# Cross-attention of a two-layer decoder: input rows normalised by ScalarE instead of VectorE, mean and root prepared as two-tensor products

## The reference

```python
q_in = _layernorm(decoder_hidden, gamma, beta)
kv_in = _layernorm(encoder_output, gamma, beta)
q = q_in @ Wqkv[:D_MODEL].T
k = kv_in @ Wqkv[D_MODEL:2 * D_MODEL].T
v = kv_in @ Wqkv[2 * D_MODEL:].T
...
scores = jnp.einsum('bhqd,bhkd->bhqk', q, k) * SCALE
scores = scores + _temporal_bias(L_q, L_kv)[None, None, :, :]
attn = jax.nn.softmax(scores, axis=-1)
attended = jnp.einsum('bhqk,bhkd->bhqd', attn, v)
attended = attended.transpose(0, 2, 1, 3).reshape(B, L_q, D_MODEL)
attended = attended @ Wout.T + b_out
gate = jax.nn.sigmoid(attended @ Wgate.T + b_gate)
output = gate * attended + (1.0 - gate) * residual
```

## Time and profile before

| what | value |
|---|---|
| median of 3 runs | 2562.7 us (2561.79 to 2567.87) |
| the profiled execution | 2562.45 us, span of its instructions 2560.6 us |
| busy in the span: TensorE, VectorE, ScalarE, GpSimd | 2133.6, 1537.1, 949.2, 926.3 us |
| the stage of the change | about 1579 to 2364 us of the span |
| mean granted TensorE clock | 0.878 of full speed |

### The profile page before, as it was taken

The page is one execution under the profiler, slowest core; times in us unless marked ns, Lnnn a source line. Parts: engine busy times, 40 slices in busy tenths (PEclk is TensorE's granted clock), DMA queues, the critical chain, the costliest instruction groups (busy, mean ns, idle before and its releaser), DMA issues. The chain is left out here.

```text
span 2560.6 us, 58413 instructions
## 1 busy us (share of the span) xinstructions
PE 2133.6 (83%) x20310; PEld 1601.6 (63%) x20310; DVE 1537.1 (60%) x3500; ACT 949.2 (37%) x1881; POOL 926.3 (36%) x911
## 2 busy tenths in 40 slices
PE   5999997999776664888399996899999999997575
PEld 4666665777676563665398885566666666664233
DVE  0344443555454455333244654699999999984798
ACT  0444442333211110333124341344444444442797
POOL 0111111111144545232554531355555555553333
PEclk9999998999887776899677887899999999997555
DMA  6011003656311110876322311011000110000111
GB/s 207 26 30 30 29 25 116 217 198 215 132 50 32 37 35 24 271 241 182 92 86 78 102 39 39 26 32 32 26 28 30 32 32 30 24 20 8 53 57 46
DMA packets 157644, 192.76 MB, mean 75 GB/s; under 512 B 28517, under 2 KB 141160, under 8 KB 157559
## 3 DMA queue, kind: packets, MB, share of 16 engines
q1 hardware_dynamic: 136426, 179.73, 22.5%
q10 hardware_dynamic: 10861, 9.30, 1.2%
q0 software_dynamic: 10272, 2.62, 0.5%
HBM read 140.74 MB, written 77.51 MB: 85 GB/s over the span
## 5 line engine op out<-in xcount | busy, mean ns | idle before, releaser
L2730 ACT ACTIVATE xa_prob<-xa_A 121x1600 f32<-121x1600 f32 x96 | 144.5, 1505 | 304.2 <-PE xa_A L2609 304.2
L2801 POOL TENSOR_TENSOR xa_prob<-xa_prob,xa_exp_bias 121x1600 f32<-121x1600 f32 x64 | 228.7, 3574 | 41.0 <-ACT xa_prob L2730 40.9
L2908 DVE TENSOR_REDUCE xa_kq<-xa_A 100x4 f32<-100x1444 f32 x128 | 211.6, 1653 | 20.8 <-PE xa_A L2582 20.6
L1408 POOL DMA_INDIRECT slot_rows<-rt_x_again,rt_slot_u x150 | 151.9, 1012 | 163.8 <-DVE rt_x_again L1526 102.1
L2888 DVE TENSOR_SCALAR xa_rows_n<-xa_rows_t,xa_mv,xa_rstd 121x256 f32<-121x256 f32 x128 | 142.4, 1172 | 2.4 <-POOL xa_rstd L2818 2.4
L2609 PEld LDWEIGHTS xa_A<-xa_q2T,xa_kqT 17*121 17x121 f32 x3072 | 93.8, 185 | 56.5 <-DVE xa_kq L2908 35.9
L2582 PE MATMUL xa_A<-xa_kqT 16*100 16x361 f32 x1024 | 112.9, 510 | 10.0 <-ACT xa_prob L2730 6.8
L2609 PE MATMUL xa_A<-xa_q2T,xa_kqT 17*121 17x100 f32 x3072 | 109.3, 280 | 13.8 <-DVE xa_kq L2908 13.2
L695 DVE TENSOR_REDUCE sa_kq<-sa_A 100x16 f32<-100x1600 f32 x32 | 58.5, 1827 | 102.8 <-PE sa_A L453 102.8
L1654 POOL DMA_INDIRECT contrib<-ex_y,ex_place_u x64 | 62.4, 975 | 154.3 <-ACT ex_y L1706 135.5
L2823 POOL TENSOR_TENSOR xa_o_rstd<-xa_o_var,xa_power 100x1 f32<-100x1 f32 x32 | 17.9, 560 | 252.1 <-DVE xa_o_var L2948 252.1
(11 more groups left out here) (345 smaller groups left out, 5439.6 us busy)
## 6 DMA issues: line engine op xcount, KB each, us to landing
ex_w<-in_w13T SPq DMA_DIRECT2D x64, 352.0 KB
contrib<-xs_zero SPq DMA_DIRECT2D x30, 640.0 KB
la_rows<-contrib SPq DMA_DIRECT2D x16, 1200.0 KB
xs_ctxT<-in_ctxT SPq DMA_DIRECT2D x32, 512.0 KB
xa_rows_t<-in_ctx SPq DMA_DIRECT2D x96, 121.0 KB
ex_w<-in_w2T SPq DMA_DIRECT2D x64, 176.0 KB
slot_rows<-xs_zero SPq DMA_DIRECT2D x32, 272.0 KB
ex_x_t<-slot_rows SPq DMA_DIRECT2D x64, 136.0 KB, 2.2
```

Of the source, the lines that this page charges most:

```text
L1408: nc.gpsimd.indirect_dma_start(slot_rows, bass.IndirectOffsetOnAxis(slot_u[:, k, n:n + 1], 0), x_again[:, k, :], None, bounds_check=SLOTS ...
L2730: nc.scalar.activation(prob[:, n, :].rearrange("p (h a) -> p h a", h=HPG), A[:ROWS, :, 0:G * T], ACT.Exp, scale=EXP_SCALE).then_inc(exp_re ...
L2801: nc.gpsimd.tensor_tensor(chunk, chunk, exp_bias[:, n, :].unsqueeze(1).to_broadcast([ROWS, HEADS, T]), ALU.mult).then_inc(biased, 1)
L2908: nc.vector.tensor_reduce(kq[:T, k, NCH, 4 * j:4 * j + 4, DH:DH + 1].rearrange("p h o -> p (h o)"), A[:T, :, 0:src_len], axis=AXIS_X, op=A ...
```

## The change

The four operations of `normalise` move from VectorE to ScalarE, as an Identity activation with `rstd` as scale and a new tile `shift` as bias. VectorE prepares `shift` = -mean x root: `nmean` (zero minus mean) in `moments`, and the product with the root in `centre`, which stands where `normalise` stood. `var` becomes a sum of two tensors, the variance and a tile filled with epsilon, instead of a tensor and a number. On ScalarE `normalise(b+3)` stands between `y_out(b-1)` and `exponential(b, 2)`. GpSimd fills two small constant tiles once.

```diff
--- before.py
+++ after.py
@@ -2412,6 +2412,10 @@
         mv = s.sb("mv", [ROWS, LOTS, 2])
         var = s.sb("var", [ROWS, LOTS])
         rstd = s.sb("rstd", [ROWS, LOTS])
+        nmean = s.sb("nmean", [ROWS, LOTS])
+        shift = s.sb("shift", [ROWS, LOTS])
+        nothing = s.sb("nothing", [ROWS, LOTS])
+        ln_eps = s.sb("ln_eps", [ROWS, LOTS])
         power = s.sb("power", [ROWS, LOTS])
         o_stats = s.sb("o_stats", [T, 6])
         o_mv = s.sb("o_mv", [T, 2])
@@ -2428,7 +2432,8 @@
         loaded = [s.sem(f"loaded{k}") for k in range(2)]
         res_loaded = [s.sem(f"res_loaded{k}") for k in range(2)]
         stored = [s.sem(f"stored{k}") for k in range(2)]
-        stats_ready, mv_ready, var_ready, rstd_ready, normed = (s.sem(n) for n in ("stats_ready", "mv_ready", "var_ready", "rstd_ready", "normed"))
+        stats_ready, mv_ready, var_ready, rstd_ready, shift_ready, normed = (s.sem(n) for n in (
+            "stats_ready", "mv_ready", "var_ready", "rstd_ready", "shift_ready", "normed"))
         turned, rowsT_ready = s.sem("turned"), s.sem("rowsT_ready")
         projected, roped, summed = s.sem("projected"), s.sem("roped"), s.sem("summed")
         kq_turned, kqT_ready = s.sem("kq_turned"), s.sem("kqT_ready")
@@ -2700,7 +2705,7 @@
             @block.scalar
             def _(act):
                 for sem, per in ((rowsT_ready, KC), (kqT_ready, G), (q2_ready, 1), (exp_ready, NCH), (v_ready, 2), (oT_ready, 1), (yT_ready, 1),
-                                 (th_ready, 1)):
+                                 (th_ready, 1), (normed, 1)):
                     act.sem_inc(sem, per * LEAD)
                 act.wait_ge(w_in, W_ALL)
                 act.wait_ge(cleared, 2)
@@ -2723,6 +2728,16 @@
                     act.wait_ge(av_done, at(b, NCH, NCH))
                     act.wait_ge(y_turned, at(later(b, -1), 1, 1))
                     nc.scalar.activation(oT[:].rearrange("p g t -> p (g t)"), CA[:, 0:G * T], ACT.Copy).then_inc(oT_ready, 1)
+
+                def normalise(b):
+                    k = b[1] % 2
+                    act.wait_ge(loaded[k], loads_of(b, LOTS))
+                    act.wait_ge(shift_ready, at(b, 1, 1))
+                    act.wait_ge(turned, at(later(b, -2), KC, KC))
+                    for n in range(LOTS):
+                        last = nc.scalar.activation(rows_n[:, k, n, :], rows_t[:, k, n, :], ACT.Identity, scale=rstd[:, n:n + 1],
+                                                    bias=shift[:, n:n + 1])
+                    last.then_inc(normed, 1)
 
                 def exponential(b, n):
                     act.wait_ge(shifted, at(b, NCH, n + 1))
@@ -2772,6 +2787,8 @@
                         values_first(later(b, 1))
                     if has(-1):
                         y_out(later(b, -1))
+                    if has(3):
+                        normalise(later(b, 3))
                     if has(0):
                         exponential(b, 2)
                     if has(1):
@@ -2784,12 +2801,15 @@
                         for j in range(1, G):
                             kq_out(later(b, 2), j)
 
+                normalise((0, 0))
                 periods(act, NB, FIRST, LAST, REACH, body)
 
             @block.gpsimd
             def _(pool):
                 for sem, per in ((rstd_ready, 1), (summed, 1), (biased, NCH - 1), (less_ready, 1), (o_rstd_ready, 1)):
                     pool.sem_inc(sem, per * LEAD)
+                nc.gpsimd.memset(nothing[:], 0.0)
+                nc.gpsimd.memset(ln_eps[:], LN_EPS)
                 nc.gpsimd.memset(power[:], -0.5).then_inc(power_set, 1)
                 nc.gpsimd.memset(v1[:], 1.0).then_inc(v_set, 1)
                 pool.wait_ge(power_set, 1)
@@ -2848,7 +2868,7 @@
 
             @block.vector
             def _(dve):
-                for sem, per in ((stats_ready, 1), (mv_ready, 1), (var_ready, 1), (normed, 1), (roped, 2), (max_ready, G), (last_biased, 1),
+                for sem, per in ((stats_ready, 1), (mv_ready, 1), (var_ready, 1), (shift_ready, 1), (roped, 2), (max_ready, G), (last_biased, 1),
                                  (rec_ready, 1), (y_ready, 1), (dg_ready, 1), (dif_ready, 1), (r_ready, 1), (o_stats_ready, 1),
                                  (o_mv_ready, 1), (o_var_ready, 1), (out_ready, 1)):
                     dve.sem_inc(sem, per * LEAD)
@@ -2878,16 +2898,14 @@
                     last.then_inc(mv_ready, 1)
                     dve.wait_ge(mv_ready, at(b, 1, 1))
                     dve.wait_ge(rstd_ready, at(later(b, -1), 1, 1))
-                    nc.vector.tensor_scalar(var[:], mv[:, :, 1], LN_EPS, None, ALU.add).then_inc(var_ready, 1)
-
-                def normalise(b):
-                    k = b[1] % 2
+                    dve.wait_ge(shift_ready, at(later(b, -1), 1, 1))
+                    nc.vector.tensor_tensor(var[:], mv[:, :, 1], ln_eps[:], ALU.add)
+                    nc.vector.tensor_tensor(nmean[:], nothing[:], mv[:, :, 0], ALU.subtract).then_inc(var_ready, 1)
+
+                def centre(b):
                     dve.wait_ge(rstd_ready, at(b, 1, 1))
-                    dve.wait_ge(turned, at(later(b, -2), KC, KC))
-                    for n in range(LOTS):
-                        last = nc.vector.tensor_scalar(rows_n[:, k, n, :], rows_t[:, k, n, :], mv[:, n, 0:1], rstd[:, n:n + 1],
-                                                       ALU.subtract, ALU.mult)
-                    last.then_inc(normed, 1)
+                    dve.wait_ge(normed, at(later(b, -1), 1, 1))
+                    nc.vector.tensor_tensor(shift[:], nmean[:], rstd[:], ALU.mult).then_inc(shift_ready, 1)
 
                 def rope(b, half):
                     dve.wait_ge(projected, at(b, 2, half + 1))
@@ -2973,7 +2991,7 @@
                     if has(1):
                         maxima(later(b, 1), 2)
                     if has(3):
-                        normalise(later(b, 3))
+                        centre(later(b, 3))
                     if has(-1):
                         differ(later(b, -1))
                     if has(1):
@@ -2981,8 +2999,9 @@
                     if has(0):
                         apply_bias(b)
 
+                dve.wait_ge(power_set, 1)
                 moments((0, 0))
-                normalise((0, 0))
+                centre((0, 0))
                 periods(dve, NB, FIRST, LAST, REACH, body)
 
 ROUND = 12582912.0
```

## The result

The changed kernel takes 2701.4 us (median of 4 runs, 2693.03 to 2709.05). The kernel before took 2562.24 us beside it (2556.24 to 2567.87), so the ratio is 1.0538, 95% interval 1.0508 to 1.0567: slower by 139 us. The forecast was slower, 2820 us, with a range of 2640 to 2920. The range holds the result, but the number is 119 us too high, and the forecast's own part of the range (2745 to 2920) does not hold it. The profiled execution took 2698.84 us, with a span of 2697.1 us (2560.6 before) and a mean granted clock of 0.849 (0.878 before).

The account below looks back on a forecast made before the run. With TensorE and VectorE near full, the order of one cross-attention batch was taken to decide. 2562.45 us plus 78 (longer chain), 6 (filling) and 174 (TensorE's clock) gave 2820 us, range 2640 to 2920.

Parts of the forecast that it names:

- the forecast's own part of the range: Whole kernel: the outcome with `shift` held and TensorE's clock falling every batch, 2745 to 2920 us; chance 0.70.
- `shift` is held: VectorE's small product waits until GpSimd's `apply_bias` 1 ends: about 3.0 us instead of 0.16.
- its nearest row: Linear-attention trace: a 128x8 two-input VectorE operation under a GpSimd operation took 2.77 us, ending 0.03 us after it.
- The chain: One cross-attention batch's waits, through `shift`, normalisations and third exponential: 25.44 us, +2.69 a batch, +78 us over 29 batches.
- The filling: Two filling bodies: `normalise` ahead of the `kqT` copies on ScalarE costs +6 us in all (0 to 8).
- TensorE's clock: A 3.6 us gap before `score` j = 3 halves the clock every batch: 6.0 us each (3.4 to 9.5), +174 us.
- rival (1): Cross-attention batches: `shift` held, but TensorE's clock stays at 1.00 or its loss hides in other waits: 2646 us; chance 0.17.
- The clock that stays up: Cross-attention batches: TensorE's clock stays at 1.00 despite the held `shift` and gap, 2646 us; chance 0.17.
- The clock that stays low into the next projections: TensorE's clock stays low beyond `keys_first`: over 2922 us; chance 0.05.
- `shift` slipping through: On VectorE `shift` slips past GpSimd in 0.16 us: batch 22.53 us, kernel 2562 us, no change; chance 0.08.

Follow-up runs that it names:

- e1: The change with `shift` made by GpSimd right behind the root instead of by VectorE: 2419.7 us, ratio 0.998 to the kernel before.
- e2: The change with `shift` on VectorE as four 121x1 operations with a number per partition, not one two-tensor product: 2443.6 us, ratio 1.0071 to the kernel before.
- e3: The change with ScalarE's `normalise` behind the third exponential, value copy and first `kqT` copy: 2430.3 us, ratio 1.0014 to the kernel before.
- e5: The change with 14 unread matmuls filling TensorE's gap before `score` j = 3: 2509.7 us, ratio 1.0334 to the kernel before.
- e9: The change with the fourth ScalarE normalisation moved behind `kq_out` 0, `shift` still on VectorE: 2701.9 us, ratio 1.0537 to the kernel before.
- e10: The change with one extra ScalarE normalisation, into an unread tile, ahead of the four: 2704.5 us, ratio 1.0555 to the kernel before.
- e8: The change with GpSimd's `residual` ahead of its `apply_bias` 1 instead of behind it: 2668.6 us, ratio 1.0973 to the kernel before.
- e11: The change with VectorE's `shift` and its wait for the root moved ahead of maximum j = 2: 2756.0 us, ratio 1.0761 to the kernel before.

## Why the prediction was right, and where not

- **`shift` is held.** Right. Forecast to end 0.03 us after GpSimd's `apply_bias` 1; it ended 0.02 after, with a median of 2.94 us. e1, e2 and e3 each remove one condition of the hold's cost, and the loss goes with each. The rule of the Trainium skill that the forecast set beside its nearest row ("GPSIMD Engine Reference", Key points: two SBUF inputs contend) agrees with these rows; "Advanced Engine Details and Errata", VectorE Performance Modes, which names two-port instructions only, would have missed it.
- **The chain.** Right to a tenth. `score_turned` n = 1 to `score` j = 3: forecast 12.91, measured 12.83 (1996.65 to 2009.48). ScalarE's normalisations to its exponential: 1.98 forecast, 1.98 measured (2005.97 to 2007.95). From `score` j = 0 on: 2.95 and 6.10 forecast, 2.95 and 6.10 measured (2014.87, 2017.82, 2023.92). TensorE's idle time: 3.6 forecast, 3.62 measured. The full-clock body of 25.44 us was seen in e5 as 25.42.
- **The filling.** Right. Forecast +6 us. The fourth root, with which the first of the 29 bodies begins, starts 64.59 us after the stage's start in the kernel before and 70.95 in the change: +6.4. The other 3.5 us of the 9.9 in the table's first column belong to that first body, whose gap of 4.1 us ends 3.2 us ahead of the column's end.
- **TensorE's clock, the term that was wrong in size.** "I take 6.0, near the middle", with bounds of 3.4 and 9.5. It falls in every body, as forecast, but costs 1.9 us a body, less than the lower bound: 29 x 4.1 = 119 us, the whole error. The lower bound counted 6.8 us at half clock as 3.4 us lost. In fact the low stretch (2007.7) begins 1.8 us before the gap ends (2009.48), so only 5.0 us of work fall in it, and some of what it delays was waited for anyway. With the measured term the sum is 2562.45 + 78 + 6 + 55 = 2701.5, against 2698.84 for the profiled execution. That the stated range held the result was luck in part: 2701 lies between rival (1)'s 2646 and the forecast's 2745, where no mechanism had been priced. The step itself, so much work at half clock and so much lost, was also too simple: in e9, the change and e10 the body stayed at 27.3 us whatever its chain, so the clock's share came out as 2.35, 1.9 and 1.4 us. e8 shows that the forecast size exists, 1.7 to 7.3 us a body, but with a gap of 4.9 us.
- **The rivals.** The clock that stays up (2646) was refuted by the windows. The clock that stays low into the next projections did not come either: the low stretch ends at 2014.5, and the key projections follow `score_turned` of 2017.82. `shift` slipping through is what e2 makes true, in the change's own order, with 0.56 us instead of 0.16: 22.53 + 0.40 = 22.93 us by the rival's terms, 23.07 measured. So that order could not gain even without the hold, as the rival said.

## What to carry to other kernels

A tiny operation is as expensive as what it waits for: before moving bulk work off VectorE, look at what small two-tensor SBUF product is left there, which GpSimd operation is in progress or next when it is issued, and who stands behind its result. Make such a product on GpSimd itself, or in single-column scalar form, and let the consumer do its urgent work first. Where a gap makes the clock fall in every body of a loop, trimming half a microsecond may return nothing (e9); close the gap far enough that the clock stays up (e3, e1).

## What the hardware showed that was not expected

- Three kernels with worked-out full-clock bodies of 24.95, 25.44 and 25.93 us (the second measured as 25.42 in e5) all ran at 27.3 us a body, one fall of the clock in each.
- A VectorE two-tensor operation of 121x4, issued under a 0.72 us GpSimd operation, waited 4.19 us through three GpSimd operations that followed one another without a pause (e8); issued 0.06 us behind the start of one, it waited 3.51 us (e11).
- Scalar forms of 121x1 with the number from a tile went through under a running GpSimd operation in 0.196 to 0.202 us, 116 of 116 (e2), while the scalar form of 121x256 was held before.
- A gap of 3.1 us before `score` j = 3 was enough for the clock to fall each time (e9). A gap of 4.9 us, 1.3 us longer than the change's, lengthened low stretches to 10.2 and 17.1 us in many bodies (e8), in an order that repeated after 12 bodies.
